# The sixth group's x1 turned by DMA, its W1 layer and softmax late in group seven, and the last group in a new order

## The reference

```python
def _L0_attn_ref(x, W_qkv, W_o, log_gamma):
    q, k, v = ...            # x @ W_qkv.T, 16 heads of 16 columns
    k = _layernorm(k)
    def step(S, qkv_t):      # scan over the 64 tokens
        S = gamma * S + v_t[..., :, None] * k_t[..., None, :]
        y_t = jnp.einsum('bhde,bhe->bhd', S, q_t)
        return (S, y_t)
    return y @ W_o.T

def _L0_cond2_ref(hidden, W1, b1, v, prompt_type_ids):
    attn_in = jnp.tanh(jnp.einsum('bsd,da->bsa', hidden, W1) + b1)
    scores = jnp.einsum('bsa,a->bs', attn_in, v)
    masked_scores = jnp.where(mask, scores[:, None, :], NEG_INF)
    p = jax.nn.softmax(masked_scores, axis=-1)
    return jnp.einsum('bjl,bld->bjd', p, hidden) / cnt[..., None]

x = x + attn(cond(x, condB_deltat, ...), ...)    # called x1 below
x = x + ffn(cond2(x, ...), ...)                  # quantized with a scale from the largest value of all tokens
```

## Time and profile before

| what | us |
|---|---|
| median of 3 runs | 266.05 (265.77 to 266.1) |
| profiled execution | 266.28 |
| its span in the trace | 264.2 |
| TensorE busy | 248.9 (94%) |
| VectorE busy | 221.5 (84%) |
| ScalarE busy | 187.8 (71%) |
| GpSimd busy | 159.2 (60%) |

### The profile page before, as it was taken

How to read it: one execution, slowest core, us unless ns; L and a number is a source line. 1 busy time by engine, 2 the same in 40 slices (tenths; PEclk the granted TensorE clock), 3 DMA queues, 4 the chain that set the end, 5 groups by cost and what they waited for, 6 DMA issues and landing times.

```text
span 264.2 us, 8416 instructions
## 1 busy us (share of the span) xinstructions
PE 248.9 (94%) x3484; PEld 171.0 (65%) x3489; DVE 221.5 (84%) x483; ACT 187.8 (71%) x327; POOL 159.2 (60%) x164
## 2 busy tenths in 40 slices
PE   4999999998999999999999999978799999998994
PEld 4879688696788788788679668846444444443331
DVE  4879679789789889689779777969879999999994
ACT  5895464772796798598691665267799899819990
POOL 6898582896895795893795560032044679740670
PEclk9999999999999999999999999999999999999999
DMA  5991406709409409906925710310046698000267
GB/s 146 356 299 34 144 0 219 107 5 307 90 35 288 83 16 297 151 19 205 190 55 161 112 32 2 119 46 4 0 129 150 140 230 309 0 2 0 111 247 278
DMA packets 40870, 33.81 MB, mean 128 GB/s; under 512 B 23488, under 2 KB 31232, under 8 KB 40832
## 3 DMA queue, kind: packets, MB, share of 16 engines
q1 hardware_dynamic: 40832, 33.28, 46.4%
HBM read 19.48 MB, written 8.42 MB: 106 GB/s over the span
## 4 chain that ended last, share of the span: by engine, by line
PE 67%; ACT 13%; DVE 11%; issue 5%; DMA 1%; POOL 1%; DVEq 0%; ACTq 0%
PE psum L969 17%; PE psum L993 6%; PE psum L1008 6%; PE psum L1135 4%; PE psum L1406 4%; ACT silu L914 3%; PE psum L1141 3%; DVE arena L1784 3%; PE psum L1142 3%; DVE arena L1561 3%; PE psum L1139 2%; ACT silu L932 2%; PE psum L1387 2%; PE psum L1137 2%; PE psum L1136 2%
## 5 line engine op out<-in xcount | busy, mean ns | idle before, releaser
L1561 DVE TENSOR_TENSOR arena<-psum,xq_mem 128x512 f32<-128x512 f32 x64 | 39.7, 683 | 3.1 <-PE psum L993 3.1
L1387 PE MATMUL psum<-xq_mem,guT 128*128 128x512 bf16 x151 | 33.8, 379 | 0.3 <-DVE arena L1784 0.2
L585 POOL TENSOR_TENSOR xT_lo<-arena,xT 128x512 fp32r<-128x512 f32 x14 | 17.6, 1279 | 19.4 <-ACT xT L733 19.4
L1387 PEld LDWEIGHTS psum<-xq_mem,guT 128*128 128x128 bf16 x152 | 14.4, 98 | 19.4 <-DVE arena L1784 1.8
L1795 DVE TENSOR_REDUCE h_max<-arena 128x1 f32<-128x1024 f32 (+1 forms) x24 | 25.9, 1123 | 0.2
L914 ACT ACTIVATE silu<-psum,gu_x 128x1024 f32<-128x1024 f32 (+1 forms) x24 | 24.4, 1026 | 2.1 <-PE psum L1387 1.1
L715 ACT ACTIVATE arena<-psum,pmask 128x512 f32<-128x512 f32 x32 | 20.3, 687 | 0.5 <-PE psum L1142 0.2
L1008 PE MATMUL psum<-arena 64*32 64x128 f32 x1024 | 19.4, 274 | 0.9 <-DVE arena L1561 0.9
L1406 PE MATMUL psum<-arena,dT 128*128 128x512 bf16 x78 | 18.8, 380 | 1.3 <-DVE arena L1854 0.6
L993 PE MATMUL psum<-arena 32*64 32x128 f32 x1024 | 19.7, 278 | 0.0
L600 POOL TENSOR_TENSOR xq_mem<-kind,xq_mem 128x256 f32<-128x256 f32 x8 | 4.9, 618 | 22.4 <-DVE arena L1650 22.4
(11 more groups left out here) (251 smaller groups left out, 727.5 us busy)
## 6 DMA issues: line engine op xcount, KB each, us to landing
arena<-in_x SPq DMA_DIRECT2D x9, 512.0 KB, 4.6
x_dram<-arena SPq DMA_DIRECT2D x8, 512.0 KB, 3.2
pooled<-x_dram SPq DMA_DIRECT2D x8, 512.0 KB, 4.9
out<-pooled SPq DMA_DIRECT2D x15, 256.0 KB, 2.1
xin<-in_x_t SPq DMA_DIRECT2D x7, 512.0 KB, 5.5
cs_rows<-cs_dram SPq DMA_DIRECT2D x12, 256.0 KB, 5.5
pooled<-in_w_qkv_t SPq DMA_DIRECT2D x3, 256.0 KB, 5.3
pooled<-in_w_down SPq DMA_DIRECT2D x1, 704.0 KB, 8.1
```

The source lines that it names most:

```text
L585: pool.tensor_tensor(xT_lo[:, k, :], xrotT[:, k, :], xT[:, k, :].bitcast(F32), ALU.subtract).then_inc(xl_ok, 1)
L1387: mm = pe.matmul(in_order(o[:, 512 * half:512 * half + 512], 2 * n + half), gT[i][:, v, c, :], xq_rows(2 * n + half, c), start=(c == 0), s ...
L1561: dve.tensor_tensor(dec[:, c, r, :, :], bank[S_BANK[r]].rearrange("q (n k) -> q n k", n=PP), two_heads, ALU.mult).then_inc(dec_done, 1)
```

## The change

Six things, all in the last two groups:

1. `BY_DMA` goes from 5 to 6: x1 of group 5 is turned by DMA. ScalarE gets two `x1_planes`, SyncE two DMA transposes, GpSimd four copies; TensorE loses eight transposes and ScalarE two copies, all in group seven.
2. The W1 layer of group 5 moves behind the sums' transpose, its `score_rows` behind the values, its `softmax_scores` behind the last `low_y`, and its `exponents` behind the Q copies. The order on ScalarE and VectorE follows. The banks of these steps change (`w1_bank`, `sv_bank`, `o_bank`, `pT_bank`).
3. The projections of group 6 write to other banks, so the first waits for Q copies, and the third waits for `s_sub` of group 5.
4. In group eight `weights_turn(5)` comes before `scores(7, 1)`, and `x1_rows(6)` behind it. The four `values` stand together. Behind them come `pool_tokens(5)`, the W1 layer of group 6, `hidden_of_x`, `score_rows(6)` and `hidden_of_y`. `weights_turn(6)` and `pool_tokens(6)` stand between the projections.
5. On VectorE the softmax of group 6 follows both `y_odd`, that of group 7 follows it directly, and the largest values and the last residual come after. All four `low_y` pieces of group eight go to GpSimd (two before). On ScalarE the pooled rows of group 6 move behind the table load.
6. `pT` has two buffers, and the mask of group 7 has one of its own.

The core of the diff:

```diff
-BY_DMA = 5
+BY_DMA = 6
...
         def o_bank(g, h):
-            return bank[1 + h if g < G - 1 else 3 + 2 * h]
+            return bank[1 + h if g < G - 2 else 2 - h if g < G - 1 else 7 - 2 * h]
...
         def w1_bank(c):
-            return bank[3] if c < G - 1 else bank[2]
+            return bank[3] if c < G - 3 or c == G - 2 else bank[1] if c == G - 3 else bank[2]
...
                 if c:
-                    pool.wait_ge(s_sub, c)
+                    pool.wait_ge(s_sub, min(c, G - 2))
...
             for b in range(2):
-                pool.wait_ge(yT_ok, 4 * G - 1 + b)
-                pool.tensor_tensor(y_part(yT_lo, b, 1), y_full(G - 1, b, 1), y_part(yT, b, 1).bitcast(F32), ALU.subtract).then_inc(yl_ok, 1)
+                for half in range(2):
+                    pool.wait_ge(yT_ok, 4 * G - 3 + 2 * b + half)
+                    pool.tensor_tensor(y_part(yT_lo, half, b), y_full(G - 1, half, b), y_part(yT, half, b).bitcast(F32), ALU.subtract).then_inc(yl_ok, 1)
...
                 if g == G - 2:
                     weights_t(c)
-                    exponents(g - 1)
+                    hidden_tanh(g - 1)
+                if g == G - 1:
+                    hidden_tanh(g - 1)
+                else:
+                    y_even(g, 1)
+                y_high(g, 1)
                 if g == G - 1:
                     pooled_rows(c)
+                    hidden_tanh(g)
+                    exponents(g - 1)
                     weights_t(g - 1)
...
-                if p == 2 and g < G - 1:
+                if p == (0 if g == G - 2 else 2) and g < G - 1:
                     pe.wait_ge(q_ok, 2 * DC * (g + 1) + 2)
+                if p == 2 and g == G - 2:
+                    pe.wait_ge(s_sub, g)
...
                 project_v(g)
-                if g > BY_DMA:
+                if g == G - 1:
+                    pe.wait_ge(q_ok, 2 * DC * g + 2 * DC)
+                    weights_turn(c)
+                scores(g, 1)
+                if g == G - 1:
                     x1_rows(g - 1)
-                scores(g, 1)
...
                 if g == G - 1:
                     pe.wait_ge(v_ok, PP * g + PP)
                     pool_tokens(c - 1)
-                    weights_turn(c)
-                    hidden_layer(g - 1)
-                    score_rows(g - 1)
...
+                    if g == G - 2:
+                        pe.wait_ge(kT_ok, DC * (g + 1) + DC)
+                        hidden_layer(g - 1)
                     values_pair(1, 0)
                     values_pair(1, 1)
+                    if g == G - 2:
+                        score_rows(g - 1)
...
                     values_last(0, 0)
                     values_last(0, 1)
-                    hidden_of_x()
+                    values_last(1, 0)
+                    values_last(1, 1)
                     pe.wait_ge(pl_cp, 2 * c)
                     pool_tokens(c)
-                    weights_turn(g - 1)
-                    values_last(1, 0)
-                    values_last(1, 1)
-                    pe.wait_ge(pl_cp, 2 * g - 2)
-                    pool_tokens(g - 1)
+                    hidden_layer(g - 1)
+                    hidden_of_x()
+                    score_rows(g - 1)
                     hidden_of_y()
                     project(g, 0)
 
             score_rows(G - 1)
+            weights_turn(G - 2)
             project(G - 1, 1)
+            pe.wait_ge(pl_cp, 2 * (G - 2))
+            pool_tokens(G - 2)
             project(G - 1, 2)
             project(G - 1, 3)
             weights_turn(G - 1)
...
                 if g == G - 1:
+                    softmax_sums(c)
+                    softmax_weights(c)
+                    y_odd(g, 0)
+                    y_odd(g, 1)
+                    largest_rows(c - 1)
                     softmax_scores(g - 1)
-                    y_odd(g, 0)
-                    largest_rows(c - 1)
                     softmax_sums(g - 1)
                     softmax_weights(g - 1)
-                    low_y(g, 0)
+                    softmax_scores(g)
+                    largest_rows(c)
```

More of the change, by code:

```diff
@@ L99, in build @@
         sm, ex = (carve(PP * S).rearrange("p (n l) -> p n l", n=PP) for _ in range(2))
-        pn, pT = (carve(PP * S).rearrange("p (q j) -> p q j", q=2) for _ in range(2))
+        pn, *pT = (carve(PP * S).rearrange("p (q j) -> p q j", q=2) for _ in range(3))
         tanhT = carve(TG // 2)
@@ L148, in build @@
         early = xq_mem[:, :].bitcast(F32)
-        mask = early[:, 0:PP * S].rearrange("p (n l) -> p n l", n=PP)
         decay = early[:, PP * S:PP * S + NH * S].rearrange("p (h t) -> p h t", h=NH)
@@ L153, in build, with mask_of @@
         base = early[:, at_d + DC * IC * P // 2:at_d + DC * IC * P // 2 + 5 * S].rearrange("p (k l) -> p k l", k=5)
+        at_m = at_d + DC * IC * P // 2 + 5 * S
+        masks = [early[:, i:i + PP * S].rearrange("p (n l) -> p n l", n=PP) for i in (0, at_m)]
+        def mask_of(c):
+            return masks[c == G - 1]
         def cols_of(u, c):
@@ L593, in cols @@
                     return base[:, k, :].unsqueeze(1).to_broadcast([P, PP, S])
+                mask = mask_of(c)
                 if c:
-                    pool.wait_ge(s_sub, c)
+                    pool.wait_ge(s_sub, min(c, G - 2))
                 else:
@@ L859, in _ @@
                     weights_t(c)
-                    exponents(g - 1)
+                    hidden_tanh(g - 1)
+                if g == G - 1:
+                    hidden_tanh(g - 1)
+                else:
+                    y_even(g, 1)
+                y_high(g, 1)
                 if g == G - 1:
                     pooled_rows(c)
+                    hidden_tanh(g)
+                    exponents(g - 1)
                     weights_t(g - 1)
-                y_even(g, 1)
-                y_high(g, 1)
-                if g == G - 1:
-                    hidden_tanh(g)
-                    pooled_rows(g - 1)
                 if g + 1 < G:
                     q_copies(g + 1, 1)
+                if g == G - 2:
+                    exponents(g - 1)
                 if g == 3:
@@ L1028, in pool_tokens @@
                             rows = slice(S * b, S * b + S)
-                            weights = pT[rows, q, e * S:e * S + S]
+                            weights = pT[c % 2][rows, q, e * S:e * S + S]
                             if c >= TURNED:
@@ L1096, in hidden_of_x @@
             def hidden_of_x():
-                pe.wait_ge(s_sub, G - 1)
+                pe.wait_ge(x1T0_ok, G - 1)
                 pe.wait_ge(xin_in, 16 * (G - 1))
@@ L1266, in _ @@
                         project_whole(K_BANK, 1, 0, k_mm)
-                        if g == G - 2:
-                            pe.wait_ge(s_sub, c + 1)
-                            score_rows(g - 1)
                         if g >= 3:
@@ L1279, in _ @@
                             weights_turn(c)
-                            pe.wait_ge(s_sub, g)
-                        elif g >= 2:
+                        if g >= 2:
                             pe.wait_ge(s_sub, c + 1)
@@ L1647, in softmax_scores @@
                 rows = sv_bank(c)[:, 0:PP * S].rearrange("p (n l) -> p n l", l=S)
-                cstep(c, 1, dve.tensor_tensor(rows, rows, mask, ALU.add))
+                cstep(c, 1, dve.tensor_tensor(rows, rows, mask_of(c), ALU.add))
                 cstep(c, 2, dve.tensor_reduce(sm_c[:, 0, :], rows, AX.X, ALU.max))
@@ L1732, in _ @@
                     low_y(g, 0)
-                y_odd(g, 1)
+                if g < G - 1:
+                    y_odd(g, 1)
                 if g == 0:
@@ L1737, in _ @@
                     low_y(g, 1)
+                if g == G - 2:
+                    softmax_scores(g - 1)
                 if g + 1 < G:
                     newton(g + 1, 1 if g else None)
-                else:
+                residual(g, 0)
+                if g == G - 1:
+                    softmax_sums(g)
+                    softmax_weights(g)
                     dve.wait_ge(pl_mm, G - 1)
```

55 lines of the change are left out of this document (17 added, 38 removed).

## The result

The changed kernel takes 263.87 us (median of 6 runs, 263.62 to 265.23) against 265.89 for the kernel before, run beside it (6 runs, 265.69 to 266.1): a ratio of 0.994, with a 95% interval from 0.9923 to 0.9956. (The means, 264.25 against 265.90, give this ratio; the medians alone would give 0.992, since most of the six lie low.) Its profiled execution took 265.14, with a span of 263.4.

The account below looks back on a forecast made before the run. TensorE was 94% busy, with everything waiting on the largest pooled value; VectorE's tail would release `pool_tokens(7)` 1.32 us earlier. Profiled execution 266.28 - 1.3 = 265.0, median 0.2 below: 264.7 us, range 263.9 to 266.0.

Parts of the forecast that it names:

- faster: Outcome that the changed kernel measures below 265.5 us; chance 0.77.
- Part 1: Group seven: turning x1 of group 5 by DMA takes 0.97 us off TensorE and costs nothing; turned at 154.1.
- Rival (c): Group seven: x1 turned by DMA comes late, TensorE waits at the W1 layer; 266.0 us; chance 0.09 shared with (d).
- Part 2: Group seven: W1 and softmax of group 5 done later; third projection from 162.37 to 161.25, a gain of 1.12 us.
- Part 3: Group eight, first half: second scores at 167.26, a new 0.6 us hole before the values, the 1.05 stall gone.
- Part 4: End of group eight: VectorE's queue sets the tail; `pool_tokens(7)` starts at 185.55 against 186.87, 1.32 us earlier.
- The deduction of 0.07: TensorE block sums: each block's row overlaps the next, so a block costs its length less 0.07 us.
- rival (a): End of group eight: VectorE's tail is longer through handoffs and ScalarE's queue; 265.2 to 265.9 us; chance 0.18.
- a larger gain: Whole kernel: better overlaps bring `pool_tokens(7)` 0.7 us earlier still; 263.7 to 264.2 us; chance 0.08.
- Rival (b): Hole before `pool_tokens(7)`: clock drops to 1.2 GHz, +2.3, 267.0 us; chance 0.07 with other losses, 266.6 and more.
- The point from which it decides: Behind the hole before `pool_tokens(7)`: from 1.3 us of TensorE work doubled by a lower clock, the gain is lost.
- (d): Order doesn't matter; something unseen sets `pool_tokens(7)`; 266.0 us; chance 0.09 shared with Rival (c).

Follow-up runs that it names:

- the second six: The changed kernel run once more, nothing altered, six executions: 265.05 us against 265.77 for the kernel before, ratio 0.9971.
- moved residual: The changed kernel with the last residual on VectorE moved ahead of the two largest-value steps of group 6: 262.88 us, ratio 0.989.
- group seven's part alone: The kernel before with only items 1 to 3 as far as they lie in group seven, group eight in old order: 264.45 us, ratio 0.9951.
- the hole filled: The changed kernel with eight more idle matmuls on TensorE before the wait for the last residual: 263.68 us, ratio 0.9921.
- group eight's part alone: The kernel before with only items 4 to 6, `BY_DMA` left at 5: 265.48 us against 265.74, ratio 1.0.

## Why the prediction was right, and where it was off

The forecast was 264.7, range 263.9 to 266.0, with 0.77 on faster. Faster it is, in both sets of runs. The forecast gain was 1.35 us (266.05 less 264.7); the means of the first six runs give 1.65, the medians of the second six 0.72. The median of the first six, 263.87, lies just under the range, their mean, 264.25, and the median of all twelve executions, 264.9, in it. That this is close to the forecast is luck in part, two errors that cancel: the gain was larger than summed, and the clock, at full in the forecast, falls in most executions.

**Part 1, the DMA turn.** Right in that it costs nothing; the bound was wide. The forecast had x1 turned at 154.1 at the latest, wanted at 155.29. It was turned at 150.2 and wanted at 154.81: a spare of 4.6, not 1.2. The wide term is "they landed 7.2 to 8.3 us after issue, so the second at most 9.7 us after the first issue": here they landed 4.5 and 3.4 us after issue, both within 6.0 of the first. Rival (c) had no ground here.

**Part 2, group seven.** Right in its mechanism. Forecast 1.12, measured 1.23 in the trace and 1.3 in the run of this part alone. Term by term, from one start to the next: the x1 turn that goes gave 0.88 (forecast 0.97), the stall at the second Q projection 0.50 (0.43). The new wait for `s_sub` shows as 0.20 in its row, but the third projection comes 1.78 behind the first instead of 1.43, so it cost 0.35 there (0.28) and 0.06 behind it. A term that the forecast didn't have made up for this: the two K projections, which now run without the score rows between them, take 2.96 instead of 3.17. `newton` and the residuals behind the softmax cost nothing, as taken.

**Part 3, first half of group eight.** Right: the second scores are 1.89 earlier against 1.72; the hole ahead of the values is 0.57 against 0.6; there is none ahead of the score rows. The list of holes before, on the other hand, missed two in group eight, 0.36 at 175.75 and 0.66 at 179.97. The sum didn't need them, since it builds the new order from its blocks.

**Part 4, the tail.** The mechanism was right, its start was off. From the softmax scores of group 6 to the end of the last residual the sum had 8.6 us (176.89 to 185.5) and the trace has 8.5 (176.03 to 184.54). But VectorE starts at 176.03, where the forecast, shifted by the 0.31, has 176.58. The mis-sized terms are in "From 170.98: four values 2.18, `pool_tokens(5)` 1.02, W1 layer 1.01, `hidden_of_x` 1.01". The 128 values in one row took 1.95 instead of twice 1.09, the W1 layer 0.92, and `hidden_of_x` 0.86 up to the next start: 0.23, 0.09 and 0.15. The score rows behind them took 0.43 instead of 0.59. The deduction of 0.07 fits blocks of different shapes; the values, and the blocks marked 128*64 in the rows, put next to their like, took less. Not all of this reached the end, since the step that VectorE then waited for was ScalarE's: the sums of group 6 start at 177.95, 0.51 before the forecast (178.77, shifted 178.46). ScalarE's row began with the tanh of group 6 at 174.71, 0.29 early by the values and what lay ahead. The tanh of group 7 started when the pooled rows let it, at 177.12, and not 1.13 behind `hidden_of_y`, at 176.92. This is what rival (a) feared, and it cost 0.2. In all `pool_tokens(7)` came 1.96 earlier instead of 1.32. The bracket of "a larger gain", 263.7 to 264.2, is where the four executions at full clock lie or nearly so (263.62 to 263.94); its chance (0.08) was too small.

**The clock.** Rival (b) came true in 8 of 12 executions, against a chance of 0.07, and with the mechanism and the place that it named: the hole ahead of `pool_tokens(7)`, 2.24 us (forecast 2.1). The argument against it, that the profile is at full clock throughout and the work on either side is dense, was worth nothing: before, the longest hole behind the kernel's start was 1.05. The Trainium skill, page "TensorE: Matmul & The Clock Gate", section "HAM oscillation — how this bites in real kernels", has it that holes in TensorE's work drop its clock to half. The trace agrees as to the half, with 0.50 granted behind a hole of 2.22. The page speaks of longer holes than this one; here the measurement decides. After the holes of 1.02 (moved residual) and 1.05 (before, and group seven's part alone) the traces show no such fall.

What kept the time down was the price. The forecast let all the work double, +2.3; it is 1.3 to 1.4. From the start of `pool_tokens(7)` to the first product it is 4.66 us with the hole filled, and 6.09 and 5.99 in the two traces at the low clock: 1.43 and 1.33 more. It is paid in two pieces, which make up that difference to within 0.06. The pooling is longer, 1.76 and 1.99 instead of 1.09, and VectorE's local largest value (L1762, with the hole filled L1764) is ready 2.91 and 3.15 us behind its start instead of 2.43: 0.48 and 0.72. Then TensorE, still in its idle matmuls at the low clock, takes that value up late: at 188.57, when it was ready at 187.51, while with the hole filled it is ready at 187.23 and taken up at 187.28. That is 1.0 in the profile after, 0.66 in the other trace. So the larger piece in the profile after is paid for matmuls whose results nobody reads. (The row of these matmuls has five of six, here as in the kernel before.)

So the loss of 1.3 ate into a gain of 2.1 and didn't turn it round. The point from which it decides, 1.3 us of doubled work, was right for the summed gain and wrong for the true one.

Rivals (c) and (d) are out by the traces: no wait for the turned x1, and `pool_tokens(7)` moved as the sum says.

## What to carry to other kernels

When a change closes small holes and collects the rest in one place, ask what that one hole does to the clock. Count its price only for the work directly behind it, and compare it with the gain: here -2.1 for the order, +1.3 for the clock. In the changed kernel eight filling matmuls bring the whole gain back, and one step moved ahead in the queue of the engine that makes the hole brings more. With group eight's part alone the filling took the low band away, but no gain in time was seen. And of several steps in a tail, those that nobody waits for stand behind the one that another engine waits for: a largest value of 1.29 us stood ahead of a residual of 0.68, and this alone cost 0.8 us.

## What the runs showed of the hardware

- A hole of 2.22 to 2.24 us in TensorE's work, between dense stretches, was followed by a lower mean clock (0.993 to 0.994) in 2 of 6 and 6 of 6 executions of the changed kernel, and in 6 of 12 of group eight's part alone, on a different chip from the six of six. In the others it stayed at 0.999 or more. Two low executions were traced, and both show 0.50 granted. What decides it in one execution is open. With holes of 0.49 to 1.02 at this place (traced) none of 29 executions was in that band; one of them, at 0.995, has no trace.
- The clock is whole in the hole itself. In both traces it falls as the pooling begins (whole to 184.5, half from 185.0) and is back at about 188.0 to 188.3, so that the work behind a wait pays for it a second time.
- Two DMA transposes of x1 landed 4.5 and 3.4 us after their issues, and those of the group before, in the kernel before, 7.2 to 8.3.
- The last store of the output landed after 1.5 us of SyncE's waiting in eight traces and after 2.1 in one. Such a step behind the last work moves the total by as much as some of the changes studied here.
